# Second experts of a two-layer gated block: the last four experts' rows are added to the stored result by the scatter itself

## The chip, the cores and the metric

The kernel runs on one core of a Trainium2 chip. A core has TensorE (matrix products), VectorE, ScalarE, GpSimd and SyncE (SP), each with its own instruction queue, and 16 DMA engines that all queues share. The engines are ordered only by semaphores. The metric is the device time of one execution in microseconds; before the change it was 932.16 us, the median of 3 runs (931.07 to 935.5).

## The reference

The input x holds 32 x 128 tokens of width 128. Four blocks follow, each added to x through a gate: a cross attention, a mixture of 64 experts with a shared one, a second cross attention, and a mixture of 8 experts in which each expert chooses its 1024 tokens of 4096. Only the last one matters here:

```python
scores = softmax(xt @ Wr)                     # xt: the normalised tokens, 4096 x 128
G, idx = top_k(scores.T, 1024)                # 8 experts, each its 1024 tokens
h = gelu(einsum('ekd,edh->ekh', xt[idx], W1) + b1)      # 1024 x 512 per expert
X_e = einsum('ekh,ehd->ekd', h, W2) + b2                # 1024 x 128 per expert
out = zeros((4096, 128)).at[idx.reshape(-1)].add(G[..., None] * X_e)
x = x + tanh(g_ffn[1]) * out
```

A token can be chosen by several experts, or by none; within one expert no token stands twice.

## The kernel before

The blocks run one after the other. The last one is `experts1_block` (L1607 to L1889); X, the running result of all tokens, lies in SBUF as 128 x 32 x 128 numbers. The rows of the normalised tokens lie in HBM in the table `token_rows`. A second table, `expert_sums`, has a row of 128 numbers for every pair of token and expert and was set to zero during the second attention.

For each expert e from 0 to 7:

- VectorE makes the list of its 1024 tokens with TensorE's help (`make_list`, lists are made three experts ahead).
- GpSimd gathers the 1024 rows with 8 indirect DMAs of 128 rows (`gather`, L1782), two experts ahead.
- VectorE takes the gates out of the rows (`gates`, L1842). TensorE turns the rows (`turn`, L1704), multiplies by W1 (`hidden`, L1715), ScalarE applies gelu (L1763), TensorE multiplies by W2 (`out`, L1727). `hidden` and `out` work in two halves, s = 0 and 1.
- VectorE adds the bias and multiplies by the gate (`scale`, L1854 and L1856), into one of two buffers `y1[e % 2]`.
- GpSimd scatters the 1024 rows into the table `expert_sums` with 8 indirect DMAs (`place`, L1792). Rows of tokens that the expert did not choose stay zero.
- SP, once all of them have landed, reads the expert's share of the table back as a dense 2 MB tile, in four parts of 512 KB (`load_sums`, L1667), into the tiles XT (even experts) and XS (odd ones).
- VectorE adds it to X in four parts of 128 x 1024 (`add_sums`, L1864).

The order on each engine is the order in the code. GpSimd: gather(0), gather(1), then for each e gather(e + 2), if there is one, and place(e); so it ends with place(3), gather(6), place(4), gather(7), place(5), place(6), place(7). VectorE: gates(e), make_list(e + 3), scale(e, 0), scale(e, 1), add_sums(e - 1), the last for e from 1 to 5; the additions of experts 5, 6 and 7 stand behind everything. SP: load(e + 2), which brings the weights of an expert (L1655 to L1658), and load_sums(e); last it stores X in four parts into `out` (L1679) and waits for them.

Semaphores that the change touches: `placed[e % 2]` counts the landed scatters of the even or odd experts, `summed` the finished additions, `stored` the landed stores.

Of the kernel before, what the change touches and what calls it, by code (L numbers as in the profile page):

```python
# [19 lines left out]
ALU = mybir.AluOpType  # L20
# [1586 lines left out]
def experts1_block(nc, t, d, sem, ps):  # L1607
# [3 lines left out]
    HALF = NT // 2  # L1611
    PARTS = 4
    BP = B // PARTS
    ev = Named()
    ev.oh = sem("moe_oh")
    ev.counted = sem("moe_counted")
# [31 lines left out]
    with nc.Block() as block:  # L1648
        @block.sync
        def _(sp):  # L1650
            def load(e):
                u = e % 2
                later(sp, ev.weights, 64 * e)
                later(sp, ev.scaled, 2 * (e - 1))
                sp.dma_start(t.w1x[:, u, :], d.w1x[e]).then_inc(ev.weights, 16)  # L1655
                sp.dma_start(t.w2x[:, u, :, :].rearrange("p c d -> p (c d)"), d.w2x[e]).then_inc(ev.weights, 16)
                sp.dma_start(t.b1x[:, u, :], d.b1x[e]).then_inc(ev.weights, 16)
                sp.dma_start(t.b2x[:, u, :], d.b2x[e:e + 1, :].rearrange("o d -> (o d)").partition_broadcast(128)  # L1658
                             ).then_inc(ev.weights, 16)

            def load_sums(e):

                sp.wait_ge(ev.placed[e % 2], gathers(e))
                for q in range(PARTS):
                    later(sp, ev.sums[q], 16 * e)
                    later(sp, ev.summed, PARTS * (e - 2) + q + 1)
                    sp.dma_start(columns(e)[:, BP * q:BP * q + BP, :],  # L1667
                                 d.sums[BP * q:BP * q + BP, :, D * e:D * e + D].rearrange("b p d -> p b d")
                                 ).then_inc(ev.sums[q], 16)

            load(0)
            load(1)
            for e in range(E1):
                if e + 2 < E1:
                    load(e + 2)
                load_sums(e)
            for q in range(PARTS):
                sp.wait_ge(ev.summed, PARTS * (E1 - 1) + q + 1)
                sp.dma_start(d.out[BP * q:BP * q + BP].rearrange("b p d -> p b d"),  # L1679
                             t.X[:, BP * q:BP * q + BP, :]).then_inc(ev.stored, 16)  # L1680
            sp.wait_ge(ev.stored, 16 * PARTS)

        @block.tensor
# [91 lines left out]
        def _(pool):  # L1775
# [10 lines left out]

            def place(e):
                pool.wait_ge(ev.placing, 2 * e + 2)
                for k in range(NT):
                    if k % 4 == 0:  # L1790
                        pool.wait_ge(ev.scaled, 2 * e + k // 4 + 1)
                    nc.gpsimd.indirect_dma_start(  # L1792
                        out=d.sums_flat, out_offset=bass.IndirectOffsetOnAxis(ap=t.sum_rows[:, e, k:k + 1], axis=0),
                        in_=t.y1[:, e % 2, k, :], in_offset=None).then_inc(ev.placed[e % 2], 16)
# [3 lines left out]
            for e in range(E1):  # L1798
                if e + 2 < E1:
                    gather(e + 2)  # L1800
                place(e)

        @block.vector
        def _(dve):
# [70 lines left out]
            for e in range(E1):  # L1875
# [6 lines left out]
                if e >= 1:  # L1882
                    scale(e, 0)
                scale(e, 1)
                if 1 <= e < E1 - 2:
                    add_sums(e - 1)
            for e in range(E1 - 3, E1):
                add_sums(e)
            c.end()  # L1889


def flamingo_kernel(nc, **dram):
# [35 lines left out]
    d.choices_flat = d.choices.rearrange("b s (k d) -> (b s k) d", d=D)  # L1928
    d.sums = nc.dram_tensor("expert_sums", [B, S, E1 * D], F32, kind="Internal").ap()
    d.sums_flat = d.sums.rearrange("b s (e d) -> (b s e) d", d=D)  # L1930
    d.rows = nc.dram_tensor("token_rows", [B, S, PAY1], F32, kind="Internal").ap()
    d.rows_flat = d.rows.rearrange("b s w -> (b s) w")

# [233 lines left out]
```

## Time and profile before

| what | value |
|---|---|
| median of 3 runs | 932.16 us |
| the profiled execution | 930.74 us |
| its span | 929.0 us |
| TensorE busy over the span | 724.3 us, 78% |
| VectorE busy | 689.3 us, 74% |
| GpSimd busy | 616.2 us, 66% |
| ScalarE busy | 472.0 us, 51% |
| mean DMA traffic | 108 GB/s |

The span is the time between the first and the last instruction that the profiler saw; the execution's own time has a little around it. GpSimd is called POOL and VectorE DVE in the rows, SPq is SP's queue. A duration behind an indirect DMA of GpSimd is that of the instruction, not of its transfer; what a transfer takes is given as its landing, counted from the issue. The second experts' stage runs from about 720 us to the end.

### The profile page before, as it was taken

Reading aid. Unit: us, or ns where it says so; the run is one execution under the profiler, and the core shown is the slowest. Engines: PE = TensorE matmul, PEld = TensorE weight load, DVE = VectorE, ACT = ScalarE, POOL = GpSimd, SP = SyncE. Lnnn points to the kernel's source line nnn. Section 1 sums busy time; section 2 is a strip of 40 time slices with the busy share of each in tenths; the row PEclk is TensorE's granted clock in tenths of the full one; section 3 lists DMA queues with packets and bytes.
Section 4 is the critical chain, followed back from the end, with each engine's and each line's share of the span. In section 5 each row is a group of like instructions: output and inputs, shape, how many; then the busy total and the mean of one; then the engine's idle time right before and its main releaser. Section 6 shows DMA issues by size and latency. Waiting matters only on the chain. (4 is left out here: it accounts for less than half of the span.)

```text
span 929.0 us, 23584 instructions
## 1 busy us (share of the span) xinstructions
PE 724.3 (78%) x6243; PEld 495.0 (53%) x6243; DVE 689.3 (74%) x2193; ACT 472.0 (51%) x1688; POOL 616.2 (66%) x1113
## 2 busy tenths in 40 slices
PE   3888999999947999649999999999811479888670
PEld 1555666566533666525666666666510256567550
DVE  3787999999977465238999999999868756775333
ACT  2886888888841122125777777777700124323220
POOL 4888666666645477467888888888310466777872
PEclk9999999999975799979999999999955599999895
DMA  5211222222123333033344444433200316656568
GB/s 161 81 54 65 78 78 79 84 82 81 72 68 93 100 107 105 10 124 110 128 142 142 143 143 132 130 126 125 79 12 0 85 49 185 167 165 164 161 194 226
DMA packets 99276, 100.61 MB, mean 108 GB/s; under 512 B 24840, under 2 KB 76622, under 8 KB 99204
## 3 DMA queue, kind: packets, MB, share of 16 engines
q1 hardware_dynamic: 88852, 88.26, 29.9%
q0 software_dynamic: 6656, 9.66, 3.7%
q10 hardware_dynamic: 3696, 1.84, 0.7%
q8 instruction: 32, 0.52, 0.2%
q14 instruction: 40, 0.33, 0.1%
HBM read 60.84 MB, written 44.17 MB: 113 GB/s over the span
## 5 line engine op out<-in xcount | busy, mean ns | idle before, releaser
L580 ACT ACTIVATE P<-bank,mx 128x120 f32<-128x120 f32 x1024 | 276.6, 429 | 70.5 <-DVE mx L884 70.5
L479 PE MATMUL bank<-ident,P 128*120 128x128 f32 x1024 | 167.4, 286 | 28.6 <-ACT P L580 24.2
L479 PEld LDWEIGHTS bank<-ident,P 128*120 128x120 f32 x1024 | 106.2, 138 | 117.6 <-issue 72.4
L884 DVE TENSOR_REDUCE mx<-bank 128x4 f32<-128x480 f32 x256 | 150.4, 650 | 20.5 <-PE bank L461 17.3
L1782 POOL DMA_INDIRECT xg<-token_rows,tokens x64 | 68.7, 1074 | 64.1 <-DVE tokens L1836 45.2
L452 PE MATMUL bank<-bp,identr 128*128 128x480 f32 x256 | 87.3, 426 | 0.0
L1792 POOL DMA_INDIRECT expert_sums<-y,sum_rows x64 | 71.8, 1122 | 22.2 <-issue 19.2
L497 PE MATMUL bank<-PT,Vb 120*32 120x128 f32 x2048 | 82.3, 279 | 5.2 <-DVE PT L892 4.6
L684 POOL TENSOR_TENSOR Km<-Kf,kmask 128x480 f32<-128x480 f32 x64 | 63.1, 987 | 27.5 <-ACT Kf L564 26.8
L649 POOL TENSOR_TENSOR rstd<-rs,minus_half 128x1 f32<-128x1 f32 x128 | 72.7, 568 | 10.7
L461 PE MATMUL bank<-Km,qf 32*128 32x480 f32 x512 | 71.3, 626 | 3.0 <-POOL Km L684 2.9
L1763 ACT ACTIVATE ge<-bank,b1x 128x512 f32<-128x512 f32 x64 | 44.0, 687 | 46.8 <-PE bank L1715 46.8
L892 DVE TENSOR_SCALAR PT<-bank,kept 120x512 f32<-120x512 f32 x96 | 67.6, 730 | 0.2 <-PE bank L479 0.2
L648 POOL TENSOR_SCALAR rs<-mv 128x1 f32<-128x1 f32 x128 | 28.9, 226 | 55.3 <-DVE mv L860 55.2
L588 ACT ACTIVATE PT<-bank 120x512 f32<-120x512 f32 x64 | 41.6, 649 | 44.9 <-PE bank L479 44.9
L1727 PE MATMUL bank<-w2x,ge 128*128 128x128 f32 x512 | 64.3, 280 | 0.0
L497 PEld LDWEIGHTS bank<-PT,Vb 120*32 120x32 f32 x2048 | 48.2, 109 | 30.2 <-DVE PT L892 17.7
L1727 PEld LDWEIGHTS bank<-w2x,ge 128*128 128x128 f32 x512 | 61.0, 195 | 1.4 <-issue 1.4
L1715 PE MATMUL bank<-xgT,w1x 128*128 128x512 f32 x128 | 58.7, 612 | 0.0
L1187 POOL DMA_INDIRECT choice_rows<-yo,place_row x32 | 32.0, 1001 | 30.6 <-issue 14.8
L890 DVE COPY PT<-bank 120x512 f32<-120x512 f32 x64 | 43.0, 672 | 9.8 <-PE bank L479 9.6
L452 PE MATMUL bank<-mask,identb 128*128 128x480 bf16 x128 | 47.7, 376 | 0.2 <-ACT P L580 0.2
(236 smaller groups left out, 1648.0 us busy)
## 6 DMA issues: line engine op xcount, KB each, us to landing
expert_sums<-zeros SPq DMA_DIRECT2D x32, 512.0 KB, 3.4
choice_rows<-zeros SPq DMA_DIRECT2D x32, 384.0 KB, 2.4
yrows<-choice_rows SPq DMA_DIRECT2D x32, 384.0 KB, 3.1
XT<-expert_sums SPq DMA_DIRECT2D x16, 512.0 KB, 6.0
XS<-expert_sums SPq DMA_DIRECT2D x16, 512.0 KB, 6.1
w<-in_w13T SPq DMA_DIRECT2D x8, 704.0 KB
token_rows<-payload SPq DMA_DIRECT2D x32, 128.0 KB, 1.7
ctx<-in_ctxT SPq DMA_DIRECT2D x64, 60.0 KB, 1.9
```

The lines of the kernel that those rows point to most:

```text
L452: nc.tensor.matmul(heads(SC[r]), t.identb[:] if L == 0 else t.identr[:], part.unsqueeze(1).broadcast_to([S, G, KV]), start=(x == 0), stop= ...
L461: nc.tensor.matmul(heads(SC[r]), t.qf[rows, u, :], t.Km[rows, u, :, :], start=False, stop=True).then_inc(ev.scores, 1)
L479: mm = nc.tensor.transpose(TB[r % 2][0:KV, S * j:S * j + S], t.P[:, r, j, :], t.ident[:])
L497: mm = nc.tensor.matmul(pv_ps[32 * j:32 * j + 32, S * (r // 2):S * (r // 2) + S], t.Vb[0:KV, v, 2 * j + r // 2, 32 * (r % 2):32 * (r % 2) ...
L580: e = nc.scalar.activation(t.P[:, r, j, :], heads(SC[r])[:, j, :], ACT.Exp, bias=t.mx[:, G * r + j:G * r + j + 1], scale=-1.0)
L649: power = nc.gpsimd.tensor_tensor(t.rstd[:, k, u, :], t.rs[:, k, u, :], t.minus_half[:], ALU.pow)
L684: nc.gpsimd.tensor_tensor(t.Km[:, w, :, :], t.Kf[:, w, :].unsqueeze(1).broadcast_to([D, G, KV]), t.kmask[:].unsqueeze(2).broadcast_to([D, ...
L884: ve.tensor_reduce(t.mx[:, G * r:G * r + G], heads(SC[r]), AX.X, ALU.min).then_inc(ev.mins, 1)
L892: ve.tensor_scalar(t.PT[0:KV, r, :], TB[r % 2][0:KV, :], at_col(t.kept, i), None, ALU.mult).then_inc(ev.pt_dve, 1)
L1727: mm = nc.tensor.matmul(Y[s][:, D * k:D * k + D], t.ge[:, s, c, 128 * k:128 * k + 128], t.w2x[:, e % 2, c, :], start=(c == 0), stop=(c == ...
L1782: nc.gpsimd.indirect_dma_start(out=t.xg[:, e % 2, k, :], out_offset=None, in_=d.rows_flat, in_offset=bass.IndirectOffsetOnAxis(ap=t.tokens ...
L1792: nc.gpsimd.indirect_dma_start(out=d.sums_flat, out_offset=bass.IndirectOffsetOnAxis(ap=t.sum_rows[:, e, k:k + 1], axis=0), in_=t.y1[:, e ...
```

## The change

The result is stored once, after the sums of experts 0 to 3 are in X (PLAIN = 4), and no longer at the end. `load_sums` and `add_sums` are done for experts 0 to 3 only. The scatters of experts 4 to 7 go into `out` itself, to the rows of their tokens, with `compute_op=ALU.add`. GpSimd waits for the four stores before the first of them, in place(5), (6) and (7) for all scatters of the expert before, and at its end for the last two experts' scatters. SP issues the stores in front of the weights of expert 6. A new view `out_flat` gives `out` as 4096 rows.

```diff
--- before.py
+++ after.py
@@ -1611,6 +1611,7 @@
     HALF = NT // 2
     PARTS = 4
     BP = B // PARTS
+    PLAIN = 4
     ev = Named()
     ev.oh = sem("moe_oh")
     ev.counted = sem("moe_counted")
@@ -1668,16 +1669,22 @@
                                  d.sums[BP * q:BP * q + BP, :, D * e:D * e + D].rearrange("b p d -> p b d")
                                  ).then_inc(ev.sums[q], 16)
 
+            def store_rows():
+
+                for q in range(PARTS):
+                    sp.wait_ge(ev.summed, PARTS * (PLAIN - 1) + q + 1)
+                    sp.dma_start(d.out[BP * q:BP * q + BP].rearrange("b p d -> p b d"),
+                                 t.X[:, BP * q:BP * q + BP, :]).then_inc(ev.stored, 16)
+
             load(0)
             load(1)
             for e in range(E1):
                 if e + 2 < E1:
                     load(e + 2)
-                load_sums(e)
-            for q in range(PARTS):
-                sp.wait_ge(ev.summed, PARTS * (E1 - 1) + q + 1)
-                sp.dma_start(d.out[BP * q:BP * q + BP].rearrange("b p d -> p b d"),
-                             t.X[:, BP * q:BP * q + BP, :]).then_inc(ev.stored, 16)
+                if e < PLAIN:
+                    load_sums(e)
+                if e == PLAIN - 1:
+                    store_rows()
             sp.wait_ge(ev.stored, 16 * PARTS)
 
         @block.tensor
@@ -1786,9 +1793,19 @@
 
             def place(e):
                 pool.wait_ge(ev.placing, 2 * e + 2)
+                if e == PLAIN:
+                    pool.wait_ge(ev.stored, 16 * PARTS)
+                elif e > PLAIN:
+                    pool.wait_ge(ev.placed[(e - 1) % 2], gathers(e - 1))
                 for k in range(NT):
                     if k % 4 == 0:
                         pool.wait_ge(ev.scaled, 2 * e + k // 4 + 1)
+                    if e >= PLAIN:
+                        nc.gpsimd.indirect_dma_start(
+                            out=d.out_flat, out_offset=bass.IndirectOffsetOnAxis(ap=t.tokens[:, e, k:k + 1], axis=0),
+                            in_=t.y1[:, e % 2, k, :], in_offset=None, compute_op=ALU.add
+                            ).then_inc(ev.placed[e % 2], 16)
+                        continue
                     nc.gpsimd.indirect_dma_start(
                         out=d.sums_flat, out_offset=bass.IndirectOffsetOnAxis(ap=t.sum_rows[:, e, k:k + 1], axis=0),
                         in_=t.y1[:, e % 2, k, :], in_offset=None).then_inc(ev.placed[e % 2], 16)
@@ -1799,6 +1816,8 @@
                 if e + 2 < E1:
                     gather(e + 2)
                 place(e)
+            for e in (E1 - 2, E1 - 1):
+                pool.wait_ge(ev.placed[e % 2], gathers(e))
 
         @block.vector
         def _(dve):
@@ -1882,10 +1901,8 @@
                 if e >= 1:
                     scale(e, 0)
                 scale(e, 1)
-                if 1 <= e < E1 - 2:
+                if 1 <= e <= PLAIN:
                     add_sums(e - 1)
-            for e in range(E1 - 3, E1):
-                add_sums(e)
             c.end()
 
 
@@ -1928,6 +1945,7 @@
     d.choices_flat = d.choices.rearrange("b s (k d) -> (b s k) d", d=D)
     d.sums = nc.dram_tensor("expert_sums", [B, S, E1 * D], F32, kind="Internal").ap()
     d.sums_flat = d.sums.rearrange("b s (e d) -> (b s e) d", d=D)
+    d.out_flat = d.out.rearrange("b p d -> (b p) d")
     d.rows = nc.dram_tensor("token_rows", [B, S, PAY1], F32, kind="Internal").ap()
     d.rows_flat = d.rows.rearrange("b s w -> (b s) w")
 
```

The two places where rows move are at the end of GpSimd's and of SP's order. On GpSimd, before, from the scatters of expert 4 on (xg: gathered rows of expert 7; expert_sums: scatters; in brackets the semaphores waited for):

```order
L1792 DMA expert_sums<-y,sum_rows 32768x128 [waits moe_scaled,moe_placing]
L1792 DMA expert_sums<-y,sum_rows 32768x128 x3
L1792 DMA expert_sums<-y,sum_rows 32768x128 [waits moe_scaled]
L1792 DMA expert_sums<-y,sum_rows 32768x128 x3
L1782 DMA xg<-token_rows,tokens 128x136 [waits moe_listed,moe_gate_ready,moe_turned]
L1782 DMA xg<-token_rows,tokens 128x136 x3
L1782 DMA xg<-token_rows,tokens 128x136 [waits moe_listed]
L1782 DMA xg<-token_rows,tokens 128x136 x3
L1792 DMA expert_sums<-y,sum_rows 32768x128 [waits moe_scaled,moe_placing]
```

The same stretch in the changed kernel:

```order
L1804 DMA out<-y,tokens 4096x128 [waits moe_scaled,moe_stored,moe_placing]
L1804 DMA out<-y,tokens 4096x128 x3
L1804 DMA out<-y,tokens 4096x128 [waits moe_scaled]
L1804 DMA out<-y,tokens 4096x128 x3
L1789 DMA xg<-token_rows,tokens 128x136 [waits moe_listed,moe_gate_ready,moe_turned]
L1789 DMA xg<-token_rows,tokens 128x136 x3
L1789 DMA xg<-token_rows,tokens 128x136 [waits moe_listed]
L1789 DMA xg<-token_rows,tokens 128x136 x3
L1804 DMA out<-y,tokens 4096x128 [waits moe_scaled,moe_placed0,moe_placing]
```

The number of DMAs is the same; their target is `out`, and the first of expert 4's now waits for `moe_stored`, the first of expert 5's for `moe_placed0` too (those of experts 6 and 7 in the same way for `moe_placed1` and `moe_placed0`). On SP, the last rows before (XS: expert 7's rows read back):

```order
L1667 DMA XS<-expert_sums 128x8x128 [waits moe_summed,moe_sums_loaded0,moe_placed1]
L1667 DMA XS<-expert_sums 128x8x128 [waits moe_summed,moe_sums_loaded1]
L1667 DMA XS<-expert_sums 128x8x128 [waits moe_summed,moe_sums_loaded2]
L1667 DMA XS<-expert_sums 128x8x128 [waits moe_summed,moe_sums_loaded3]
L1679 DMA out<-X 128x8x128 [waits moe_summed] x4
L1648 UNCONDITIONAL_BRANCH [waits moe_stored]
```

The same store in the changed kernel, between the last read of expert 3's rows (XS) and the weights of expert 6 (w1x, w2x, b1x, b2x) and 7 (the first of them is the last row):

```order
L1668 DMA XS<-expert_sums 128x8x128 [waits moe_summed,moe_sums_loaded3]
L1676 DMA out<-X 128x8x128 [waits moe_summed] x4
L1656 DMA w1x<-in_w1x 128x512 [waits moe_scaled,moe_weights]
L1657 DMA w2x<-in_w2x 128x512
L1658 DMA b1x<-in_b1x 128x4
L1659 DMA b2x<-in_b2x 128x128
L1656 DMA w1x<-in_w1x 128x512 [waits moe_scaled,moe_weights]
```

The stores of X moved from the end to before the weights of expert 6, and no reads of `expert_sums` follow them. On VectorE the sixteen instructions of L1864 for experts 4 to 7 are gone and nothing else moves.

## Rows read from the trace of the kernel before

**Rows 1.** By stretch: TensorE, its loads, VectorE, ScalarE, GpSimd; then clock, DMA share, GB/s.
```profile
860.00:900.00 40.00, 31.80 (x175) 23.77 (x173) 11.32 (x15) 12.19 (x18) 31.24 (x29) 0.91 0.56 167
900.00:929.00 29.00, 0.00 (x0) 0.00 (x0) 14.88 (x14) 0.00 (x0) 10.41 (x7) 0.56 0.82 235
```

**Rows 2.** Chain of waits at the end: start us, us, what.
```profile
911.27 2.25 DMA expert_sums<-y,sum_rows
...
915.62 7.09 DMA XS<-expert_sums
...
922.73 1.23 DVE X L1864
```

**Rows 3.** GpSimd in order of time: start us, us, instruction, [idle before].
```profile
852.82 2.00 POOL L1792 DMA_INDIRECT expert_sums<-y,sum_rows  x1 [0.30 <-issue]
855.12 0.98 POOL L1792 DMA_INDIRECT expert_sums<-y,sum_rows  x1 [0.30 <-issue]
...
864.05 0.99 POOL L1782 DMA_INDIRECT xg<-token_rows,tokens  x1 [0.30 <-issue]
...
869.10 1.80 POOL L1782 DMA_INDIRECT xg<-token_rows,tokens  x1 [0.30 <-issue]
...
877.39 1.34 POOL L1792 DMA_INDIRECT expert_sums<-y,sum_rows  x1 [0.30 <-issue]
...
901.02 1.80 POOL L1792 DMA_INDIRECT expert_sums<-y,sum_rows  x1 [0.30 <-issue]
```

**Rows 4.** GpSimd's groups from 852.8 on: xcount | busy us, mean ns | idle.
```profile
L1792 POOL DMA_INDIRECT expert_sums<-y,sum_rows x32 | 36.6, 1145 | 9.8 <-issue 9.8
L1782 POOL DMA_INDIRECT xg<-token_rows,tokens x8 | 10.9, 1362 | 2.4 <-issue 2.4
```

**Rows 5.** VectorE in order of time, same columns.
```profile
852.72 1.23 DVE L1864 TENSOR_TENSOR X<-X,XS 128x1024 f32<-128x1024 f32 x1 [1.02 <-DMA XS<-expert_sums]
...
868.85 1.22 DVE L1864 TENSOR_TENSOR X<-X,XT 128x1024 f32<-128x1024 f32 x1 [6.63 <-DMA XT<-expert_sums]
...
877.17 0.69 DVE L1856 TENSOR_TENSOR y<-y,gs 128x512 f32<-128x512 f32 x1
...
896.63 0.69 DVE L1856 TENSOR_TENSOR y<-y,gs 128x512 f32<-128x512 f32 x1
...
900.15 0.69 DVE L1856 TENSOR_TENSOR y<-y,gs 128x512 f32<-128x512 f32 x1
900.76 4.63 DVE L1864 TENSOR_TENSOR X<-X,XS 128x1024 f32<-128x1024 f32 x4
```

**Rows 6.** SP's queue in order of time.
```profile
846.36 1.98 SPq L1655 DMA_DIRECT2D w1x<-in_w1x  x1
...
918.63 5.73 SPq L1679 DMA_DIRECT2D out<-X  x4
```

**Rows 7.** SP's waits from 900 on: us in total, times, longest.
```profile
SPq L1648 <- DMA out<-X: 4.2, 1, 4.2
```

**Rows 8.** By tile, min/median/max: scatters (ns), landing of out, of XS (us); first gathers (ns).
```profile
L1792 POOL DMA_INDIRECT expert_sums<-y,sum_rows x64: 965/971/1997, 761.5 to 911.3; - x64
...
DMA to landing us min/median/max: 4.6/5.0/5.4
...
DMA to landing us min/median/max: 3.8/6.1/9.5
...
L1176 POOL DMA_INDIRECT xp<-token_rows,place_tok x32: 994/999/1423, 286.0 to 366.7; - x32
```

**Rows 9.** TensorE in order of time.
```profile
860.58 7.03 PE L1715 MATMUL bank<-xgT,w1x 128*128 128x512 f32 x16
...
878.77 1.97 PE L1704 MATMUL bank<-ident,xg 128*128 128x128 f32 x8 [7.58 <-DMA xg<-token_rows,tokens]
```

**Rows 10.** DMA issues between 889 and 899: xcount, median us to landing.
```profile
expert_sums<-y,sum_rows POOLq DMA_INDIRECT x8, 5.7
```

**Rows 11.** DMA queue of GpSimd between 852 and 864: packets, MB, share.
```profile
q0 software_dynamic: 318, 0.66, 16.6%
```

## The prediction

> **What bounds the kernel now.** I read the profile from its end backwards. The profiled execution took 930.74 us, 1.74 us of it outside its span of 929.0 us, and lies 1.42 us under the median of the runs shown, 932.16 us. The change touches only the last 80 us, so I cut those into stretches [rows 1]: between 860 and 900 every engine works, after 900 TensorE is silent, while VectorE and the DMA engines (82%) run.
>
> The chain of waits [rows 2] says why. Expert 7's last scatter starts at 911.27 and lands 2.25 us later. Then its rows are read back, the last part 7.09 us after its issue, added by VectorE, and stored. From the landing, 913.53, to 929.0 nothing but this tail runs: 15.5 us.
>
> Before 911.27 the chain is GpSimd alone. Its timeline [rows 3] shows no idle time but 0.30 us between instructions: scatters of expert 4 from 852.82, gathers of expert 7 from 864.05, scatters of expert 5 from 877.39, then of experts 6 and 7. From the first of these to 911.27 are 39 steps in 58.45 us. An undisturbed step is 0.97 (the median scatter [rows 8]) + 0.30 = 1.27 us; 39 of them are 49.5. So 8.9 us are something else. The busy times agree: 36.6 + 10.9 = 47.5 us for 40 instructions, against 40 × 0.97 = 38.8 [rows 4]. The long instructions tell what it is. The scatter at 852.82 takes 2.00 us and ends 0.87 us after VectorE's addition of 852.72 to 853.95; the gather at 869.10 takes 1.80 us and ends 0.83 us after that of 868.85 to 870.07; the scatter at 901.02 takes 1.80 us under the four from 900.76 [rows 3, 5]. GpSimd's indirect DMAs stand still while VectorE adds tiles of 128x1024.
>
> The Trainium skill, page "SBUF — State Buffer", section "Who interferes with whom", infers the opposite: a tensor_tensor would take only the read side of the ports shared with GpSimd and leave descriptor generation alone. The rows just named contradict it. By that rule nothing of the 8.9 us would come back (rival D).
>
> **The change part by part.**
>
> 1. The tail goes: minus 15.5 us [rows 2].
>
> 2. Sixteen additions and sixteen reads of 512 KB go, those of experts 4 to 7, and with them their hold on GpSimd: minus 8.9 us. The multiplications of `scale` stay and hold it too, for less: the scatter at 877.39 took 1.34 us under the one at 877.17 [rows 3, 5]. For those I put 0.5 us back, bounds 0 and 8 × 0.37 = 3.
>
> 3. The new wait of `place(4)` for the stores. Expert 3's last addition ends at 852.72 + 1.23 = 853.95 [rows 5]. The same pattern, additions behind arriving parts and each part's store behind its addition, stands in the old tail: the last addition ends at 923.96 [rows 2], SP's last issue at 924.36, and SP waits 4.2 us more [rows 6, 7], to 928.6, so 4.6 us from addition to landing. That gives 858.6, with the wake-up 858.8, instead of 852.82: plus 6.0 us. Bounds: a store lands 4.6 to 5.4 us after its issue, a read among other traffic up to 9.5 [rows 8], so 6 to 11. Behind the waiting scatter stand expert 7's gathers, and for them waits TensorE's `turn(7)`. They now run from 858.8 + 8 × 1.27 = 869.0 to 879.2; before, 864.05 to 877.39, since the additions of expert 4 held them. TensorE idles 7.58 us for them already [rows 9]; that becomes 9.4. `scale(7, 0)` and `scale(7, 1)`, which ended at 897.3 and 900.8 [rows 5], move by the same 1.8 us to 899.1 and 902.6. By the sum below they are wanted at 904 and 909: hidden by 5 and 6 us. The weights of expert 6 pass behind the stores on SP's queue, from 846.36 [rows 6] to about 854.4; `hidden(6)` started at 860.58 [rows 9] and may slip a few us, which vanish in the same 9 us of idle time. Cost 0; without that cover, what it slips.
>
> 4. `place(5)` waits for expert 4's scatters, long landed, since eight gathers lie between. `place(6)` and `place(7)` wait for the scatters straight before them: a landing plus 0.1 us takes the place of a step of 1.27.
>
> 5. The landing of an adding scatter; no row shows one. Lower bound: a plain one, 2.25 us [rows 2]. Upper bound: 5.7, the median of plain scatters beside big reads [rows 10]. I take 3.5, nearer to the lower row since the queues are empty now: the old row must be read first, and I price the read at what a plain scatter needs behind its instruction, 2.25 − 0.97 = 1.28 us. Two waits: 2 × (3.5 + 0.1 − 1.27) = plus 4.7. At the end the landing is 1.25 us longer than the one in the old chain, and about 0.3 us lie between it and the end of the span: plus 1.6.
>
> 6. GpSimd's own time for an adding scatter: 32 of them, all on the chain; no row shows one. An indirect DMA takes about the same whatever it moves: a scatter of 512 B rows 0.97 us, a gather of 544 B rows 0.99, a gather of 1024 B rows 1.00 [rows 3, 8]. But all have 128 rows, so a price per row can't be seen. Lower bound 0.97, upper bound 1.97, a held scatter at its longest [rows 8]. I take 0.97, the row of the nearest kind: cost 0, bound 32 × 1.0 = 32 us.
>
> 7. The DMA engines. Between 852 and 864 the software queue's 318 packets took 16.6% of 16 engines × 12 us = 31.9 us, 0.10 us each [rows 11]; a scatter, at 4 rows a packet 32 of them, keeps each engine busy for 0.2 us of a step of 1.27. Up to six times that is hidden. Cost 0.
>
> Sum: −15.5 − 8.9 + 0.5 + 6.0 + 4.7 + 1.6 = −11.6 us. 930.74 − 11.6 = 919.1 for the profiled execution, 920.5 as a median. What a measurement of this kernel can tell from no change is about 0.5%, 4.7 us.
>
> **The rivals.**
>
> A. The adding scatter costs GpSimd half as much again, 1.46 us: 32 × 0.485 = plus 15.5, giving 936.0, no change. For it: a price per row would look constant here. Against it: doubling a row's bytes moved an instruction by 0.03 us at most. Beside it, the Trainium skill, page "Collectives: The Full Stack", section "The bandwidth ceiling: the fold count and why AG ≠ RS ≠ AR", says that a copy that reduces emits two reads per chunk where a plain one emits one; three descriptors in place of two would be this ratio. No row here shows it.
>
> B. Slower: each adding scatter makes a step of 2.27 us, because GpSimd takes 1.97 for it or because the engines need over ten times their present 0.2 us: plus 32, giving 952.5. It cancels the gain from 11.6 / 32 = 0.36 us more per scatter on, and is slower by over 0.5% from 0.51. For it: the rows show the engines only copying, never reading, adding and writing a row; against: the reserve of six times.
>
> C. Part of such a price, 0.1 to 0.3 us per scatter (plus 3.2 to 9.6), or landings of 5.7 (3 × 2.2 = plus 6.6): 924 to 930. The near equality of the three kinds of row speaks against the first, the empty queues against the second.
>
> D. The holds aren't VectorE's doing and stay: 920.5 + 8.9 = 929.4. The three pairs of ends above speak against it.
>
> E. The lower bounds hold: landing 2.25 (3 × 1.25) and no hold left (0.5): 916.2.
>
> **How the numbers follow.** The forecast with E, 915 to 924: 48%. C 15%: 11% faster, 4% (above 927.5) the same. A 12%: 9% the same, 3% slower. B 22%, slower. D 3%, the same. So faster 0.59, same 0.16, slower 0.25. The range 914 to 941 leaves out B and little else; the forecast's own range is 915 to 926.
>
> **What would show it.** On GpSimd: an idle stretch of 6 us before the first adding scatter, ended near 858.8 by the stores; adding scatters of 0.97 us; two idle stretches of 2 to 3 us before the first scatters of experts 6 and 7; nothing near 2 us after 854; the last scatter near 913.6 and nothing behind its landing. Wrong it would be with adding scatters at 1.3 us or more, with idle time spread between them, with a landing over 6 us, or with `scale(7, 1)` as what releases the last scatters.

## The result, and the profile after

The changed kernel took 943.01 us (median of 4 runs, 941.58 to 943.96), the kernel before beside it 933.46 us: ratio 1.0102, 95% interval 1.007 to 1.0134. It is slower by 1.0%, where 920.5 was forecast, and lies above the range. Runs more than 1.5% above the fastest of their kernel are left out of every ratio here. Its profiled execution took 943.96 us, with a span of 942.2 us, 13.2 more than before.

The stretches from 860 on, with the columns of [rows 1], show that GpSimd stays busy to the end, while VectorE and the DMA engines have less to do than before and some of TensorE's work has moved behind 900:

```profile
860.00:900.00 40.00, 26.31 (x126) 19.90 (x126) 4.44 (x8) 9.55 (x15) 31.59 (x23) 0.79 0.39 60
900.00:942.00 42.00, 9.88 (x71) 8.25 (x69) 2.77 (x4) 2.78 (x5) 27.09 (x18) 0.67 0.32 28
```

GpSimd in order of time (start, duration, engine, line, operation, idle time before it and what ended it), the instructions that answer to [rows 3]: the first scatter of expert 4, the second, the last two of expert 5, the first of experts 6 and 7, and the very last one:

```profile
861.70 1.62 POOL L1804 DMA_INDIRECT out<-y,tokens  x1 [8.25 <-issue]
863.62 1.57 POOL L1804 DMA_INDIRECT out<-y,tokens  x1 [0.30 <-issue]
...
899.06 1.56 POOL L1804 DMA_INDIRECT out<-y,tokens  x1 [0.30 <-issue]
900.92 1.56 POOL L1804 DMA_INDIRECT out<-y,tokens  x1 [0.30 <-issue]
904.95 1.56 POOL L1804 DMA_INDIRECT out<-y,tokens  x1 [2.46 <-issue]
...
922.01 1.56 POOL L1804 DMA_INDIRECT out<-y,tokens  x1 [2.47 <-issue]
...
935.04 1.56 POOL L1804 DMA_INDIRECT out<-y,tokens  x1 [0.30 <-issue]
```

An adding scatter takes 1.56 us where a plain one took 0.97, and the 0.30 us between two are the same. The waits are where they were expected: 8.25 us for the stores, 2.46 and 2.47 us before the scatters of experts 6 and 7. One of the forecast's signs didn't come: the third scatter still took 2.06 us, 0.50 above its own 1.56, under a multiplication of `scale`. GpSimd first, then VectorE:

```profile
865.49 2.06 POOL L1804 DMA_INDIRECT out<-y,tokens  x1 [0.31 <-issue]
```
```profile
865.42 0.69 DVE L1875 TENSOR_TENSOR y<-y,gs 128x512 f32<-128x512 f32 x1
```

Its groups of instructions from the first adding scatter on answer to [rows 4]:

```profile
L1804 POOL DMA_INDIRECT out<-y,tokens x32 | 50.8, 1588 | 22.0 <-issue 22.0
L1789 POOL DMA_INDIRECT xg<-token_rows,tokens x8 | 7.9, 985 | 2.4 <-issue 2.4
```

The view of the tile `out`, as in [rows 8]:

```profile
L1804 POOL DMA_INDIRECT out<-y,tokens x32: 1554/1558/2056, 861.7 to 935.0; - x32
L1676 SPq DMA_DIRECT2D out<-X x4: 651/756/1454, 848.5 to 854.8; - x4
...
DMA to landing us min/median/max: 3.2/3.3/7.4
```

32 adding scatters kept GpSimd busy for 50.8 us; 32 × 0.97 would be 31.0. They land 3.3 us after their issue. The gathers of expert 7 are free of long instructions (7.9 us for 8, against 10.9). The software queue from 900 on, 18 adding scatters, answers to [rows 11]:

```profile
q0 software_dynamic: 2604, 1.18, 33.6%
```

2604 packets took 33.6% of 16 × 40 us, so each scatter 145 packets and 0.75 us of each engine, against 32 packets and 0.2 us before: more than three times as much, but still inside a step of 1.86 us. By size they are 16 small packets and 128 of 512 B, so one for each row; the plain scatters of the first experiment below make 16 small ones and 16 of 4 KB. The last addition of expert 3, behind which the last store stands, in VectorE's order of time, as in [rows 5]:

```profile
853.55 1.23 DVE L1883 TENSOR_TENSOR X<-X,XS 128x1024 f32<-128x1024 f32 x1 [0.91 <-DMA XS<-expert_sums]
```

And SP's order of time, as in [rows 6], the four stores in one row and the first load of expert 6's weights behind them:

```profile
848.50 7.76 SPq L1676 DMA_DIRECT2D out<-X  x4
856.35 1.32 SPq L1656 DMA_DIRECT2D w1x<-in_w1x  x1
```

Side by side, by the forecast's own terms (us):

| stretch | forecast | measured | difference |
|---|---|---|---|
| end of expert 3's last addition | 853.95 | 854.78 | +0.8 |
| from there to the first adding scatter | 4.85 | 6.92 | +2.1 |
| first to last scatter | 54.7 | 73.34 | +18.6 |
| last scatter to the end of the span | 3.8 | 7.16 | +3.4 |
| end of the span | 917.3 | 942.2 | +24.9 |

### The profile page after: what moved, and what is told of

It is laid out like the page before. It is cut to its first block and busy times, and to the rows that moved or that the text cites. A ratio compares the mean times of both kernels' runs of the same rounds, so it can differ in the third digit from the quotient of the medians.

```text
span 942.2 us, 23522 instructions
## 1 busy us (share of the span) xinstructions
PE 731.1 (78%) x6243; PEld 500.6 (53%) x6243; DVE 669.4 (71%) x2177; ACT 471.9 (50%) x1688; POOL 627.0 (67%) x1113
## 5 line engine op out<-in xcount | busy, mean ns | idle before, releaser
L1789 POOL DMA_INDIRECT xg<-token_rows,tokens x64 | 65.5, 1024 | 63.8 <-DVE tokens L1855 44.9
L1734 PE MATMUL bank<-w2x,ge 128*128 128x128 f32 x512 | 67.5, 289 | 0.0
L1804 POOL DMA_INDIRECT out<-y,tokens x32 | 50.8, 1588 | 22.0 <-issue 22.0
L1734 PEld LDWEIGHTS bank<-w2x,ge 128*128 128x128 f32 x512 | 64.2, 204 | 1.4 <-issue 1.4
L1873 DVE TENSOR_TENSOR y<-bank,b2x 128x512 f32<-128x512 f32 x16 | 11.1, 692 | 63.1 <-PE bank L1734 49.1
```

What stands on the lines that cost most here:

```text
L1734: mm = nc.tensor.matmul(Y[s][:, D * k:D * k + D], t.ge[:, s, c, 128 * k:128 * k + 128], t.w2x[:, e % 2, c, :], start=(c == 0), stop=(c == ...
L1789: nc.gpsimd.indirect_dma_start(out=t.xg[:, e % 2, k, :], out_offset=None, in_=d.rows_flat, in_offset=bass.IndirectOffsetOnAxis(ap=t.tokens ...
L1804: nc.gpsimd.indirect_dma_start(out=d.out_flat, out_offset=bass.IndirectOffsetOnAxis(ap=t.tokens[:, e, k:k + 1], axis=0), in_=t.y1[:, e % 2 ...
```

## The experiments

They ran on different chips. On one kind the kernel before takes about 930 us, on another about 995; each kernel is compared with the kernel before on its own chip.

**The addition taken out of the scatters.**

```diff
-                            in_=t.y1[:, e % 2, k, :], in_offset=None, compute_op=ALU.add
+                            in_=t.y1[:, e % 2, k, :], in_offset=None
```

> The changed kernel with the addition taken out of the scatters (they overwrite the rows of the result, so the output lacks sums). Theory: the addition itself is what makes a scatter of experts 4 to 7 take GpSimd 1.56 us, so they fall to 0.97, 32 x 0.59 = 18.9 us less, the landing falls from 3.3 to 2.25 (three of them exposed, 3 us), and the time is 921 us. Rival: the target (the output tensor, hardware-wise another buffer than the table) or the other list of rows makes them slow; then they stay at 1.56 and the time stays at 943.

920.79 us, ratio 0.9881 (0.9835 to 0.9926). The view of the tile `out` in this kernel:

```profile
L1804 POOL DMA_INDIRECT out<-y,tokens x32: 963/969/1484, 856.5 to 911.4; - x32
...
DMA to landing us min/median/max: 2.2/2.2/6.8
```

The first and the last of its scatters, in GpSimd's order of time:

```profile
856.51 0.99 POOL L1804 DMA_INDIRECT out<-y,tokens  x1 [7.85 <-issue]
...
911.45 0.96 POOL L1804 DMA_INDIRECT out<-y,tokens  x1 [0.30 <-issue]
```

0.969 us and a landing of 2.2: the addition makes the price, not the target or the list. The time is the forecast's 920.5, and so is the ratio (920.5 / 932.16 is 0.9875). Term by term the agreement is partly luck. The last addition of expert 3 ended at 849.97, 4.0 us before the 853.95 of the forecast; from there to the first scatter were 6.54 us, not 4.85, and from the last scatter to the end of the span 6.05, not 3.8. First to last scatter are 54.94 us, as in the forecast's 54.7, though the landing is 2.2 and not 3.5: the two waits are steps of 3.00 us, 1.2 less together than forecast, and GpSimd idles once more, before the second scatter of expert 6, for which the trace names no cause:

```profile
889.25 0.97 POOL L1804 DMA_INDIRECT out<-y,tokens  x1 [2.03 <-issue]
891.90 0.97 POOL L1804 DMA_INDIRECT out<-y,tokens  x1 [1.67 <-issue]
```

**VectorE's additions of experts 4 to 7 taken out of the kernel before.**

```diff
-                    later(sp, ev.summed, PARTS * (e - 2) + q + 1)
+                    later(sp, ev.summed, PARTS * (min(e, 5) - 2) + q + 1)
...
-                sp.wait_ge(ev.summed, PARTS * (E1 - 1) + q + 1)
+                sp.wait_ge(ev.sums[q], 16 * E1)
+                sp.wait_ge(ev.summed, PARTS * 3 + q + 1)
...
-                if 1 <= e < E1 - 2:
+                if 1 <= e < 5:
                     add_sums(e - 1)
-            for e in range(E1 - 3, E1):
-                add_sums(e)
```

> The kernel before, with VectorE's additions of experts 4 to 7 left out and their reads kept (the output lacks those experts). Theory: VectorE's additions hold GpSimd's indirect DMAs, so none of about 2 us is left after 854 and the last scatter starts at 902 to 903 instead of 911.3; the tail keeps its reads and stores, minus one addition, so 929 falls to about 919 in the span, 922 as a median. Rival: the traffic of the reads makes the long instructions; then they stay where reads run, the last scatter stays near 911, and only the addition of 1.2 us in the tail is missing: 931.

925.65 us, ratio 0.9932 (0.9889 to 0.9975). GpSimd in order of time: the last held scatter (under the last addition of expert 3), a gather and a scatter of the stretch in which reads still run, the first scatter of expert 7, the last scatter:

```profile
853.63 1.76 POOL L1793 DMA_INDIRECT expert_sums<-y,sum_rows  x1 [0.30 <-issue]
...
868.64 0.94 POOL L1783 DMA_INDIRECT xg<-token_rows,tokens  x1 [0.30 <-issue]
...
888.97 0.97 POOL L1793 DMA_INDIRECT expert_sums<-y,sum_rows  x1 [0.30 <-issue]
...
897.22 0.97 POOL L1793 DMA_INDIRECT expert_sums<-y,sum_rows  x1 [2.18 <-DVE y L1857]
...
906.21 0.97 POOL L1793 DMA_INDIRECT expert_sums<-y,sum_rows  x1 [0.31 <-issue]
```

No instruction over 1.16 us is left after 855, though all reads still run (SP issues those of experts 4 and 5 at 865.8 and 886.1). So VectorE's additions, not the reads, make the 2 us instructions. First to last scatter fell from 58.45 to 52.58 us, 5.9 instead of 8.9: at 897.22 GpSimd now waits 2.18 us for `scale(7, 0)`, so that 50.4 us are its own and TensorE's chain is next late. So the last scatter came at 906.2 and not at 902 to 903. The tail from it is 18.0 us, not shorter than the 17.7 before, though an addition is missing in it; a store lands after 6.2 us there, not 5.0. These two make 925.65 of the 922; why the stores landed later isn't shown.

**SP waits for the last scatters instead of GpSimd.**

```diff
             sp.wait_ge(ev.stored, 16 * PARTS)
+            for e in (E1 - 2, E1 - 1):
+                sp.wait_ge(ev.placed[e % 2], gathers(e))
...
-            for e in (E1 - 2, E1 - 1):
-                pool.wait_ge(ev.placed[e % 2], gathers(e))
```

> The changed kernel with the last wait, for the scatters of experts 6 and 7, on SP in place of GpSimd. Theory: the last scatter lands at 938.4, and the 3.8 us from there to the end of the span at 942.2 come from GpSimd waiting and closing the block; with SP waiting the span ends 0.3 to 0.5 us after the landing, 939.5 as a median instead of 943. Rival: the time belongs to the adding scatters (data still on its way that no semaphore shows) or to closing after any GpSimd DMA; then it stays 943.

940.71 us, ratio 1.0101 (1.0041 to 1.016), too wide to tell 3 us. The trace does: the last scatter starts at 932.07 and the span ends at 937.2, 5.13 us later, against 7.16 in the changed kernel. That scatter on GpSimd:

```profile
932.07 1.56 POOL L1806 DMA_INDIRECT out<-y,tokens  x1 [0.30 <-issue]
```

And in SP's waits (total, times, longest, us), what it waits for at the closing:

```profile
SPq L1649 <- PEq L1649: 1.6, 1, 1.6
```

So 2.0 of the extra 3.4 us at the end belong to GpSimd as the engine that waits and closes. The 5.13 us that are left are a landing of 3.3 and 1.8 more; 1.6 us are SP waiting for the sequencer of TensorE in the closing of the block (0.2 in the kernel before), for which the traces show no cause. The theory got 2.0 of its 3.5 us.

**Five experts as before, three with adding scatters.**

```diff
-    PLAIN = 4
+    PLAIN = 5
```

> The changed kernel with five experts as before and three with adding scatters. By the price per scatter: eight adding scatters fewer are 8 x 0.59 = 4.7 us less; the store waits behind the additions of expert 4, which end near 877, so it lands near 883 and GpSimd waits 5 us there instead of 8.3, 3 us less, but the additions of expert 4 hold the gathers of expert 7 again, 3.4 us more: 943 - 4 = 939. If the waits were what costs (a store late by much more), it is 943 or more.

938.3 us, ratio 1.0101 (1.0065 to 1.0137). GpSimd waited 7.2 us for the stores, not 5, and its 24 adding scatters took 1.55 us each. The first and the last of them in GpSimd's order of time:

```profile
873.84 1.61 POOL L1804 DMA_INDIRECT out<-y,tokens  x1 [7.20 <-issue]
...
921.29 1.55 POOL L1804 DMA_INDIRECT out<-y,tokens  x1 [0.31 <-issue]
```

That the time is the expected 939 is luck: it was counted from 943 beside a kernel before of 933.46, and here that one took 930.1. In ratios 939 would be 1.006. Measured is 1.0101, the 1.0102 of the change, and 1.006 lies just below the interval. So the 4 us are not seen, and the experiment doesn't test the price per scatter beyond the 1.55 us of its rows. Other settings of PLAIN were not run.

**What the price hangs on: half the rows, or half of each row.** Three kernels; the edit of the first, the second also without the addition, the third with `t.y1[:, e % 2, k, 0:64]` and `out` seen as rows of 64 numbers:

```diff
-out_offset=bass.IndirectOffsetOnAxis(ap=t.tokens[:, e, k:k + 1], axis=0),
-in_=t.y1[:, e % 2, k, :], in_offset=None, compute_op=ALU.add
+out_offset=bass.IndirectOffsetOnAxis(ap=t.tokens[0:64, e, k:k + 1], axis=0),
+in_=t.y1[0:64, e % 2, k, :], in_offset=None, compute_op=ALU.add
```

> The changed kernel with adding scatters of 64 rows in place of 128 (half the rows of experts 4 to 7 are left out). If the price of an adding scatter is one per row, its 1.56 us fall well below, to 0.8 to 1.1; if it is one per instruction, it stays near 1.5. Rows of the plain kind say nothing, all had 128.

> The same with plain scatters of 64 rows onto the result (overwriting; half the rows left out). If GpSimd pays per row for plain scatters too, 0.97 falls to 0.5 to 0.7; if plain scatters have a fixed price, it stays at 0.97. The difference to the adding ones of 64 rows is 0.59 us if the addition costs per instruction, 0.30 if per row.

> The changed kernel with adding scatters of 128 rows of 256 B in place of 512 B (the other half of each row is left out, and the rows go to wrong places). If the price hangs on bytes, 1.56 us falls toward 1.27; if it hangs on rows or instructions, it stays at 1.56, and only the landing of 3.3 us may shrink a little.

The line of the scatters in the view of the tile `out` (min/median/max in ns), first adding, 64 rows:

```profile
L1804 POOL DMA_INDIRECT out<-y,tokens x32: 1392/1400/1483, 912.2 to 979.3; - x32
```

Plain, 64 rows:

```profile
L1804 POOL DMA_INDIRECT out<-y,tokens x32: 891/897/1091, 907.1 to 966.5; - x32
```

Adding, 128 half rows:

```profile
L1804 POOL DMA_INDIRECT out<-y,tokens x32: 1554/1558/1987, 905.8 to 978.5; - x32
```

| rows | plain | adding | difference |
|---|---|---|---|
| 128 | 0.969 | 1.558 | 0.589 |
| 64 | 0.897 | 1.400 | 0.503 |

On a straight line through the two sizes, the only ones measured, a row costs 0.072 / 64 = 1.1 ns plain and 0.158 / 64 = 2.5 ns adding. The other 0.82 and 1.24 us are then paid by the instruction. Of the 0.59 us, 0.42 are fixed and 0.17 grow with the rows. Half the bytes of a row change nothing for an adding scatter. What in the instruction takes the fixed part isn't shown. Each of the three kernels ran once, on the slower chip (987.80, 974.12 and 987.13 us, where the kernel before took 991.82); that says nothing on the time.

**Adding scatters without the waits**, into the zeroed table instead of the result.

```diff
-                if e == PLAIN:
-                    pool.wait_ge(ev.stored, 16 * PARTS)
-                elif e > PLAIN:
-                    pool.wait_ge(ev.placed[(e - 1) % 2], gathers(e - 1))
...
-out=d.out_flat, out_offset=bass.IndirectOffsetOnAxis(ap=t.tokens[:, e, k:k + 1], axis=0),
+out=d.sums_flat, out_offset=bass.IndirectOffsetOnAxis(ap=t.sum_rows[:, e, k:k + 1], axis=0),
```

> The changed kernel with the adding scatters of experts 4 to 7 sent to the zeroed table expert_sums in place of the result, and without the waits for the store and between experts, which that target doesn't need (the output lacks those experts). Theory: a scatter stays at 1.56 us, since the addition costs and not the target; the waits go, 8 us before the first and 2 x 2.2 between experts, 12 us: 943 - 12 = 931. If waits were the main cost of the change, the time would fall under 925; if the target mattered, a scatter would leave 1.56.

969.45, 971.20 and 978.08 us against 991.82 on the slower chip, ratio 0.9809 (0.9759 to 0.986); the rows are from a fourth execution, of 984.22 us. Plain and adding scatters into the same table, in the view of that tile:

```profile
L1805 POOL DMA_INDIRECT expert_sums<-y,sum_rows x32: 967/987/1969, 794.2 to 890.7; - x32
L1800 POOL DMA_INDIRECT expert_sums<-y,sum_rows x32: 1555/1559/2002, 906.0 to 975.4; - x32
```

1.559 us into this table too, so the target doesn't matter. The absolute 931 was for the faster chip, where it is a ratio of 0.998; there this kernel wasn't run. On the slower kind of chip the waits are worth more than the additions' 18.9 us: from the unaltered change (1.0048, below) to this ratio are 2.4%, some 24 us. The traces come near it: before the first adding scatter GpSimd idled 20.0 us in the change and 3.9 us here, and two waits of 2.2 us go too, 20.5 together. So on that kind the rival, waits as the main cost, holds. In the trace of the change on the faster kind the waits are 8.25 and 2 × 2.2, 12.6 us, less than the additions take. The scatter of the 3.9 us:

```profile
905.95 2.00 POOL L1800 DMA_INDIRECT expert_sums<-y,sum_rows  x1 [3.91 <-DVE y L1871]
```

**The weights of expert 6 issued behind the landed stores.**

```diff
+                if e == PLAIN:
+                    sp.wait_ge(ev.stored, 16 * PARTS)
                 if e + 2 < E1:
                     load(e + 2)
```

> The changed kernel with the weights of expert 6 issued only when the stores have landed. The stores landed 6.9 us after the last addition of expert 3 (854.8 to 861.7 with the wake-up), not the 4.65 us of the old tail. Theory: the 578 KB of weights issued behind the last store share the engines with it; with them held back GpSimd's wait ends 1.5 to 2 us earlier, 4.8 to 5.4 us after that addition. TensorE's hidden products of expert 6 start later, near 865 to 866, which vanishes in its idle time: the time is 941. Rival: the gathers and reads already under way make the store slow; then it stays at 6.5 to 7 us.

1004.45 us against 998.74, ratio 1.0064 (1.0037 to 1.0091). On this chip the additions of expert 3 ran back to back from 913.41 to 918.03, their reads long done. SP in order of time, the last store and the first instruction behind the wait for the stores:

```profile
914.66 4.30 SPq L1676 DMA_DIRECT2D out<-X  x4
924.18 0.35 SPq L1656 DMA_DIRECT2D w1x<-in_w1x  x1
```

And on GpSimd, the first scatter behind the same wait:

```profile
924.96 1.61 POOL L1806 DMA_INDIRECT out<-y,tokens  x1 [17.41 <-DMA out<-X]
```

6.9 us from the last addition to the scatter, with no weights in the way: the rival's number, but not for its reason, as no reads were under way either. 2.1 MB of stores alone need that long here, where the additions end 4.6 us after the first begins: the engines moved them from 915.3 to 923.2, at 270 to 290 GB/s. And GpSimd starts 0.8 us after SP on the same semaphore. The experiment doesn't say what made the 6.9 us in the changed kernel, where additions were spaced by reads and weights did follow. Its trace shows that the DMA engines were never idle from 848 to 861: they moved 4.2 MB of reads, stores, weights and gathered rows, and the four stores landed after 6.8 us (median), where those of the old tail took 5.0. In time, holding the weights back gained nothing (1.0064, against 1.0048 for the change as it is, on another chip of this kind).

**The additions of experts 5 to 7 held back**, in the kernel before, until GpSimd has issued its last scatter.

```diff
                 place(e)
+            pool.sem_inc(ev.all_issued, 1)
...
+            dve.wait_ge(ev.all_issued, 1)
             for e in range(E1 - 3, E1):
                 add_sums(e)
```

> The kernel before, with the additions of experts 5, 6 and 7 held back until GpSimd has issued its last scatter. Theory of the holds: expert 7's scatters no longer meet additions, so the last one starts 3.5 to 4 us earlier (907.4 against 911.3 in the trace of before); the additions of experts 5 and 6 then run while expert 7's rows are read, and the last addition ends about 2.5 us earlier than before: ratio 0.997. Rival: the additions in front of expert 7's reads and additions lengthen the tail by as much as the scatters gain; then the ratio is 1.00 or a little above.

> The kernel before with the additions of experts 5, 6 and 7 held back until GpSimd has issued its last scatter, once more: on the slower chip its ratio was 1.0005 (0.998 to 1.003), where the chain ran through TensorE and the holds fell into idle time. Theory: on a chip with the higher clock the last scatter starts 3 to 4 us earlier and the ratio is 0.997. Rival: the longer tail takes it all, and it is 1.00 there too.

999.63 against 998.74 us (1.0005, 0.9983 to 1.0027) on the slower chip, 927.72 against 931.43 us (0.9958, 0.9925 to 0.9991) on the faster. Neither tests the theory. VectorE in the second, the addition that waited for the signal:

```profile
897.99 4.63 DVE L1866 TENSOR_TENSOR X<-X,XS 128x1024 f32<-128x1024 f32 x4 [0.39 <-POOLq L1803]
```

GpSimd in the second, a held scatter and the last one:

```profile
904.91 1.97 POOL L1793 DMA_INDIRECT expert_sums<-y,sum_rows  x1 [0.30 <-issue]
907.18 1.20 POOL L1793 DMA_INDIRECT expert_sums<-y,sum_rows  x1 [0.30 <-issue]
```

The increment, queued behind the last scatter, released VectorE 9.2 us before that scatter started, only 0.39 us later than it would have gone anyway. Five of the eight scatters of expert 7 had yet to start, and three were held at 1.97 us. VectorE went on 0.4 us after the end of `scale(7, 1)`, the last thing that GpSimd's program waits for (0.55 us on the slower chip), so the increment looks bound to that wait and not to the scatters; no run separates the two. The interval that excludes 1 therefore belongs to a kernel that is all but the one before, and shows how far such an interval can be trusted here; the ratio of 0.9932 above, with as wide an interval, rests on its trace for the same reason.

**Held back in earnest:** the signal is now a one-element memset on GpSimd.

```diff
-            pool.sem_inc(ev.all_issued, 1)
+            nc.gpsimd.memset(t.table_made[:, 0:1], 0.0).then_inc(ev.all_issued, 1)
```

> The kernel before with the additions of experts 5, 6 and 7 held back until a one-element memset, queued on GpSimd behind its last scatter, has run. In the two runs before, the signal was a bare increment in GpSimd's queue; it came 9.2 us ahead of the last scatter, and the additions met the scatters as ever, so they tested nothing. Theory of the holds: now no scatter of expert 7 is held (0.97 us each), the last one starts about 54.7 us after the first of expert 4 in place of 58.45, the tail grows by 1 to 2 us, since the additions of experts 5 and 6 now lie in front of that of expert 7: 2 us less, ratio 0.998. Rival: held or not, the additions must be done behind the last store's chain, and the tail grows by 4 us or more: 1.000 or above.

> The held-back kernel once more, for the other kind of chip: on the slower one its ratio was 0.9984 (0.9961 to 1.0007). Theory of the holds: where GpSimd alone makes the chain from expert 4's scatters on, the last scatter starts 3 to 4 us earlier relative to the first of expert 4 than in the kernel before (54.7 against 58.45), the tail is 1 to 2 us longer, and the ratio is 0.998 or a little under. Rival: the tail grows by as much as the scatters gain, and the ratio is 1.000 or above.

998.0 against 999.53 us (0.9984, 0.9961 to 1.0007) and 988.24 against 990.99 us (0.9971, 0.9937 to 1.0005), both on the slower chip. GpSimd in order of time, the first scatter of expert 7 and the last one:

```profile
968.51 0.97 POOL L1793 DMA_INDIRECT expert_sums<-y,sum_rows  x1 [3.81 <-DVE y L1858]
...
977.42 0.97 POOL L1793 DMA_INDIRECT expert_sums<-y,sum_rows  x1 [0.30 <-issue]
```

VectorE, the first addition behind the signal:

```profile
978.54 4.63 DVE L1866 TENSOR_TENSOR X<-X,XS 128x1024 f32<-128x1024 f32 x4 [7.47 <-POOL table_made L1803]
```

No scatter of expert 7 is held, and first to last scatter is 66.06 us, against 69.82 in the kernel whose signal came early (on another chip of the slower kind); the tail is 20.68 against 17.93 us. So 3.8 us are gained and 2.8 given back, the theory with a longer tail than it had. It is the only version with a complete output that points below the kernel before with a mechanism shown in the trace, by 0.2 to 0.3%, and each interval still holds 1. On the faster chip it wasn't met.

**The change twice more, unaltered.**

> The changed kernel once more, unaltered, to see whether its loss hangs on the chip that it meets: on the chip of the last two groups TensorE was granted 0.74 to 0.75 of its clock between 700 and 900 us against 0.83 to 0.88 before, GpSimd idled for 3 to 5 us at a time on VectorE and TensorE, and the adding scatters of 256 B rows took 987 us against 992. Theory: the price of 32 x 0.59 us stays 18.9 us wherever GpSimd alone makes the chain, so on a chip with the higher clock the ratio is 1.010 again; on one with the lower clock part of it fills idle time and the ratio is 0.995 to 1.005. Rival: the ratio is the same on every chip.

> The changed kernel unaltered beside the held back one, to have both against the kernel before on one chip. On a chip with TensorE's granted clock near 0.9 over the kernel: ratio 1.010 to 1.012. On one where it is below 0.89 for the kernel before too: 0.995 to 1.005, since GpSimd's chain then has idle time before the stores.

941.8 against 931.43 us (1.0112, 1.0087 to 1.0138) on the faster chip, 1004.41 against 999.53 us (1.0048, 1.0023 to 1.0073) on the slower. Granted TensorE clock between 700 and 900 us: 0.82 and 0.73. What GpSimd waited for on the slower one (total, times, longest, us):

```profile
POOL out L1804 <- DMA out<-X: 20.0, 1, 20.0
...
POOL out L1804 <- DVE gs L1861: 0.3, 1, 0.3
```

And in VectorE's order of time, the second part of `scale` of expert 4 and the additions of expert 3 behind it:

```profile
915.12 0.69 DVE L1873 TENSOR_TENSOR y<-bank,b2x 128x512 f32<-128x512 f32 x1 [3.71 <-PE bank L1734]
...
916.46 4.62 DVE L1883 TENSOR_TENSOR X<-X,XS 128x1024 f32<-128x1024 f32 x4
```

20 us of idle time before the first adding scatter: the additions, and so the stores, stand behind a `scale` that waits for TensorE, whose chain is late there. From the first to the last adding scatter are 72.80 us, against 72.77 on the faster chip, so behind the stores the price of the additions is paid in full. The loss is still smaller, and a reason is seen in the kernel nearest to the one before, with the early signal, on that kind of chip: its scatters wait 16.3 us for `scale` (GpSimd's waits, 890 to 1000), and those of the changed kernel 0.3 for `gs` and nothing for `scale`.

```profile
POOL expert_sums L1793 <- DVE y L1858: 16.3, 4, 4.8
```

So first to last scatter grows by 3.0 us there (72.80 against 69.82), by 14.9 on the faster chip (73.34 against 58.45); the first scatter starts 18.4 us later (928.14 against 909.75), there 8.9. These are single executions on two chips of the slower kind, so how much each wait makes of the time isn't shown. That the loss hangs on the chip is likely: 1.0087 to 1.0138 and 1.0023 to 1.0073 don't meet, but the unaltered change ran on one slower chip only, and the interval with the early signal warns of trusting one.

## Why the prediction was wrong

- **Step 6, GpSimd's own time for an adding scatter, failed.** It was put at 0.97 us, "the row of the nearest kind: cost 0". It is 1.56 us. Of the 32 × 0.59 = 18.9 us, 29 × 0.59 = 17.1 stand between the first scatter and the last; the other three lie inside landings that step 5 had priced at 3.5 us. With the 17.1 the forecast's sum is −11.6 + 17.1 = +5.5 us, 937.7 as a median: slower by 0.6%, and inside the range. Taking the addition alone away brought the time to 920.79. So this step makes 17.1 of the 24.9 us that the span missed, and the others below are what carried the time past the range. 1.56 lay inside the bounds (0.97 to 1.97) and near rival A's price (1.46), but A was given 12% and its time of 936.0 called no change. The bound was named and the lower end taken because other plain transfers looked alike; none of them added.
- Rival A had the size and the wrong reason. A third descriptor per row would cost by the row, but half the rows take only 0.16 us off 1.56. The Trainium skill, page "Collectives: The Full Stack", section "The bandwidth ceiling: the fold count and why AG ≠ RS ≠ AR", speaks of two reads per chunk in a transfer that reduces. The 1.5 worked out from it came near the 1.6 of the whole instruction (1.558 / 0.969), but the extra time is mostly not one by the row, so the nearness is chance.
- Step 1, the tail: right in kind. It is gone, but the end costs 7.16 us after the last scatter, not 3.8; 2.0 of these 3.4 us come from GpSimd closing the kernel. The 0.3 us between a landing and the end were read off a kernel that SP closes.
- Step 2, the holds: right for the additions. With them gone from the kernel before, no instruction over 1.16 us is left. The share of `scale` was put too low: it held two scatters and a gather for 0.50, 0.32 and 0.24 us, 1.1 us and not 0.5, and one of them took 2.06 us. The Trainium skill, page "SBUF — State Buffer", section "Who interferes with whom", infers that a tensor_tensor leaves descriptor generation alone, and by that the holds would stay; by this measurement a tensor_tensor with two inputs in SBUF does hold an indirect DMA of GpSimd.
- Step 3, the wait for the stores: 8.9 us, not 6.0 (0.8 of it is a later start of everything). Two things differ from the old tail that served as its pattern: the four stores landed after 6.8 us, not 5.0, with gathers and weights on the same DMA engines, and GpSimd starts 0.8 us after SP on the same semaphore, seen on the slower chip. How the 2.1 us divide between them isn't shown.
- Step 4, the waits between experts: a step of 4.03 us, forecast 3.6. Step 5, the landing: 3.3 us, forecast 3.5; between it and the next scatter lie 0.7 us, not 0.1. The nearness of the landing is in part luck: of the 1.1 us above a plain one (3.3 against 2.2) 0.59 are the longer instruction, and 0.5 are left for what was priced as a read at 1.28. Step 7: 0.75 us of each engine, hidden as said; its "4 rows a packet" is a mean, plain scatters make packets of 8 rows and small ones. TensorE and `scale` stayed hidden: `scale(7, 1)` ended at 911.3, 18 us before the scatter that wants it (929.45).

## What to carry to other kernels

Before a transfer is given another kind, here one with an addition, its issue on GpSimd must be priced. The extra 0.59 us was mostly a fixed price per instruction, 32 of them stood on a chain that was GpSimd's alone, and together with the new waits they cost more than the 24.4 us of tail and holds that the change saved. Where no row shows a cost that multiplies by 32, the middle of its bounds, not the lower end, belongs into the sum; here the middle was 1.47 us, 0.09 off. A gain or loss in waits is only real on the engine that makes the chain, and which engine that is can differ from chip to chip: on the slower kind the scatters of a kernel like the one before wait 16.3 us for `scale`, on the faster one not at all.

## What the runs showed of the hardware that wasn't expected

- An indirect scatter costs GpSimd 0.82 us + 1.1 ns per row plain and 1.24 us + 2.5 ns per row adding (a line through 64 and 128 rows).
- A bare increment behind GpSimd's DMAs was seen by VectorE 9.2 us before the last of them started, with five of them yet to start, on both chips (970.38 and 979.57 us on the slower one); a memset's came after it.
- An adding scatter of 128 rows makes 145 packets, one for each row among them, where a plain one makes 32.
